# First stage of a fused attention and FFN kernel: row maximum taken with the bias sum, key blocks and values placed by POOL

## What is computed

```
xn = layernorm(x)                              # [32, 128, 128]
q  = xn @ Wq          -> 16 heads of 8
k  = ctx @ Wk         -> 4 groups of 8, each serves 4 heads
v  = ctx @ Wv         -> 4 groups of 8
ct = cumsum(deltas)
bias = w * log1p(abs(ct[:, None] - ct[None, :])) + (1 - mask) * -1e9
s  = q k^T / sqrt(8) + bias                    # 16 heads x 128 x 128 per batch
p  = softmax(s)
x1 = x + (p v) @ Wo
z  = layernorm(x1)                             # input of the main stage
out = x1 + main_stage(z)
```

## Time and profile before

| | us |
|---|---|
| median of three runs | 3308.8 (3306.87 to 3309.24) |
| span of the profiled execution, first to last instruction | 3304.7 |
| what the median has beyond that span | 4.1 |
| first score matmul of the first stage | starts at 17.2 |
| score matmuls of the stage's slots 3 to 32 | start at 35.97 to 292.58 |
| busy share of the whole span | PE 95%, DVE 87%, ACT 81%, POOL 74% |

### The profile page before, as it was taken

One profiled execution on the slowest core, in us unless ns is written; L12 is line 12 of the kernel. 1 busy time (PEld: TensorE's weight loads), 2 busy tenths in 40 slices (PEclk: granted clock), 3 DMA queues, 4 the chain that ended last, 5 costly groups with the idle time before them and its releaser, 6 DMA issues.

```text
span 3304.7 us, 181505 instructions
## 1 busy us (share of the span) xinstructions
PE 3125.4 (95%) x71268; PEld 2192.5 (66%) x71268; DVE 2884.0 (87%) x6045; ACT 2663.4 (81%) x5440; POOL 2447.9 (74%) x2673
## 2 busy tenths in 40 slices
PE   6776899999999999999999999999999999999996
PEld 4443567676667676676767667676676767667665
DVE  7886789999899999899999899998899999899984
ACT  6886678888788888788888788888788888788874
POOL 3333778888788888788888778787787878788883
PEclk9988999999999999999999999999999999999997
DMA  3000112122222222222222212122221212212121
GB/s 79 8 7 10 47 51 59 50 59 71 67 56 53 56 53 77 63 54 55 54 55 74 68 50 59 50 59 77 57 59 50 59 50 77 66 50 59 50 58 50
DMA packets 150374, 182.24 MB, mean 55 GB/s; under 512 B 51572, under 2 KB 74162, under 8 KB 149554
## 3 DMA queue, kind: packets, MB, share of 16 engines
q1 hardware_dynamic: 150322, 181.55, 21.2%
HBM read 21.32 MB, written 2.10 MB: 7 GB/s over the span
## 4 chain that ended last, share of the span: by engine, by line
PE 57%; issue 13%; DVE 10%; ACT 10%; POOL 5%; SPq 1%; DVEq 1%; DMA 1%; ACTq 1%; POOLq 0%
PE bank L1252 13%; PE bank L1339 8%; PE bank L1322 7%; PE bank L1262 5%; PE bank L1363 5%; PE bank L1270 3%; PE bank L1290 3%; ACT L798 3%; DVE tb L966 3%; ACT P L774 3%; PE bank L1392 2%; ACT gl L766 2%; POOL qk L524 2%; DVE bank L1075 2%; PE bank L1400 2%
## 5 line engine op out<-in xcount | busy, mean ns | idle before, releaser
L533 POOL TENSOR_TENSOR qk<-qk,rn 128x512 f32<-128x512 f32 x768 | 803.0, 1046 | 356.8 <-DVE rn L985 356.8
L524 POOL TENSOR_TENSOR qk<-ta,tb 128x512 f32<-128x512 f32 x768 | 978.6, 1274 | 2.5 <-DVE tb L966 2.5
L1252 PE MATMUL bank<-wqkv,zsT 128*128 128x512 f32 x1536 | 819.9, 617 | 25.4 <-ACT vt L705 12.3
L963 DVE TENSOR_TENSOR ta<-bank,rot 128x512 f32<-128x512 f32 x768 | 527.5, 687 | 116.1 <-ACT sq L688 87.4
L966 DVE TENSOR_TENSOR tb<-bank,rot 128x512 f32<-128x512 f32 x768 | 523.0, 681 | 0.0
L1068 DVE TENSOR_REDUCE bank<-sq 128x32 f32<-128x2048 f32 x192 | 440.6, 2295 | 25.1
L688 ACT ACTIVATE sq<-bank 128x512 f32<-128x512 f32 x768 | 445.2, 611 | 14.8 <-PE bank L1252 12.1
L696 ACT ACTIVATE qkT<-bank 128x512 f32<-128x512 f32 x768 | 396.6, 602 | 57.1 <-PE bank L1290 56.9
L1363 PEld LDWEIGHTS bank<-wo,oT 128*128 128x128 f32 x3072 | 375.4, 193 | 92.4 <-issue 92.4
L743 ACT ACTIVATE znT<-bank,small 128x128 f32<-128x128 f32 x192 | 87.9, 458 | 431.8 <-PE bank L1383 431.8
L564 POOL TENSOR_TENSOR P<-P,rowsum 128x512 f32<-128x512 f32 x384 | 392.9, 1045 | 20.0 <-DVE rowsum L1083 20.0
(11 more groups left out here) (131 smaller groups left out, 5740.6 us busy)
## 6 DMA issues: line engine op xcount, KB each, us to landing
vs<-vt SPq DMA_DIRECT2D x1152, 128.0 KB, 2.4
wqkv<-L_ffn_Wqkv SPq DMA_DIRECT2D x6, 1024.0 KB, 5.0
zm<-zm SPq DMA_DIRECT2D x192, 31.8 KB
wqkv<-L_ffn_Wqkv SPq DMA_DIRECT2D x6, 512.0 KB, 3.7
wo<-L_ffn_Wo SPq DMA_DIRECT2D x6, 512.0 KB, 4.0
z_sb<-x SPq DMA_DIRECT2D x4, 512.0 KB, 5.1
ctxb<-ctx SPq DMA_DIRECT2D x32, 64.0 KB, 1.8
w<-L_ffn_W SPq DMA_DIRECT2D x6, 341.0 KB
```

Of the source, the lines that this page charges most:

```text
L524: g.tensor_tensor(o, i0, i1, ALU.add).then_inc(s["g_add"], 1)
L533: g.tensor_tensor(q3, q3, r3, ALU.mult).then_inc(s["g_qk"], 1)
L963: v_.tensor_tensor(ta[:, c].rearrange("p (h d) -> p h d", d=DH), bank[j % 2][:, :].rearrange("p (h d) -> p h d", d=DH), rot[:, o:o + 64].u ...
L1252: t_.matmul(bank[j % 2][:, :], zsT[:, pu, :], wqkv[:, 512 * j:512 * j + 512], start=True, stop=True).then_inc(s["p_qk"], 1)
```

## The change

- `add_bias` and `maximum` become `bias_max`: per head one `tensor_tensor_reduce` of 128x128, which writes the sum of scores and bias to `XP` and the maximum over the row to one column of `xmax`. `xmax` gets two buffers.
- POOL subtracts the maxima of all four groups, in four instructions, each after its group of `bias_max`.
- ACT takes the exponentials of heads 8 to 15 in one instruction as those of 0 to 7, with no bias operand.
- ACT copies queries, keys and values of A out of bank 6 in one instruction of 288 columns to `qkvx`; the factor 1/sqrt(8) moves into the block mask `blk`.
- POOL makes `kblk` and `vaug` of A from `qkvx`, at the end of its slot.
- Two waits of PE before the transposes of A fall away, and ACT's copy waits for `vaug` of two batches before.

```
-c[:, C_BLK:C_BLK + XR] = (r[:, None] // XD) % XR == np.arange(XR)[None, :]
+c[:, C_BLK:C_BLK + XR] = ((r[:, None] // XD) % XR == np.arange(XR)[None, :]) * np.float32(XSCALE)
...
 POOL
-subtract(0)
-subtract(1)
+for gr in range(XG):
+    subtract(gr)          # waits x_add of group gr; 128x512 each
 if D_on:
     wait(pool, "x_ve", count(1, D, 1, B))
     g.tensor_tensor(rstd[:, 0:1], ve[:, 0:1], half_neg[:, 0:1], ALU.pow).then_inc(s["x_rstd"], 1)
     g.tensor_copy(x1_sb[:, bass.ds(D * E, E)], x1cur[:, :]).then_inc(s["x_store"], 1)
 if A1_on:
     deltas_of(A1, (k + 1) % 2)
+if A_on:
+    wait(pool, "x_q", count(1, A, 1, B))
+    wait(pool, "x_S", count(4, A - 2, 4, B))
+    g.tensor_tensor(kblk[:, pA, :].rearrange("p (r t) -> p r t", r=XR),
+                    qkvx[:, pA, S:2 * S].unsqueeze(1).to_broadcast([128, XR, S]),
+                    blk.unsqueeze(2).to_broadcast([128, XR, S]), ALU.mult).then_inc(s["x_kblk"], 1)
+    wait(pool, "x_O", count(1, A - 2, 1, B))
+    pool.nop(nofuse=True)
+    g.tensor_copy(vaug[:, pA, :, 0:XD], qkvx[:, pA, 2 * S:].rearrange("p (g d) -> p g d", g=XG))\
+        .then_inc(s["x_vaug"], 1)
...
 ACT, exponent(j)
-if j == 0:
-    wait(act, "x_sub", count(2, Bt, 2, B))
-    ins = a_.activation(pr, pr, ACT.Exp)
-else:
-    wait(act, "x_max", count(2, Bt, 2, B))
-    for h in range(8, 16):
-        pr = XP[:, pB, 128 * h:128 * h + 128]
-        ins = a_.activation(pr, pr, ACT.Exp, bias=xmax[:, h:h + 1])
+wait(act, "x_sub", count(4, Bt, 2 * j + 2, B))
+pr = XP[:, pB, 1024 * j:1024 * j + 1024]
+ins = a_.activation(pr, pr, ACT.Exp)
...
-a_.activation(qT[:, pA, :], bank[6][:, 0:128], ACT.Copy, scale=XSCALE).then_inc(s["x_q"], 1)
+wait(act, "x_vaug", count(1, A - 2, 1, B))
+a_.activation(qkvx[:, pA, :], bank[6][:, 0:2 * S + XG * XD], ACT.Copy).then_inc(s["x_q"], 1)
...
 DVE
-add_bias(0) ... add_bias(3)
-maximum(0)
+bias_max(gr), for gr in 0 to 3:
+    wait(dve, "x_S", count(4, Bt, gr + 1, B))
+    wait(dve, "x_sub", count(4, Bt - 2, gr + 1, B))
+    dve.nop(nofuse=True)
+    for h in range(4 * gr, 4 * gr + 4):
+        c = slice(S * (h % 4), S * (h % 4) + S)
+        ins = v_.tensor_tensor_reduce(XP[:, pB, S * h:S * h + S], bank[gr][:, c], bias[:, pB, :],
+                                      1.0, LOWEST, ALU.add, ALU.max, xmax[:, pB, h:h + 1])
+    ins.then_inc(s["x_add"], 1)
...
-maximum(1)
...
-wait(dve, "x_q", ...); v_.tensor_tensor(kblk ...)
...
-wait(dve, "x_O", ...); v_.tensor_copy(vaug ...)
...
 PE
-t_.matmul(bank[gr][:, :], qT[r, pB, :], kblk[r, pB, :], start=True, stop=True)
+t_.matmul(bank[gr][:, :], qkvx[r, pB, 0:S], kblk[r, pB, :], start=True, stop=True)
...
-wait(pe, "x_kblk", count(1, A - 1, 1, B))
-wait(pe, "x_vaug", count(1, A - 1, 1, B))
```

More of the change, by code:

```diff
@@ L42 @@
 MASKED = -(2.0 ** 120)
+LOWEST = -3.0e38
 C_ID, C_SH, C_TRI, C_ROT, C_MASK, C_SEL, C_BLK, C_END = 0, 128, 256, 384, 640, 704, 768, 772
@@ L161, in build @@
         cxT = sb("cxT", [128, 2, 2 * S])
-        qT = sb("qT", [128, 2, S])
+        qkvx = sb("qkvx", [128, 2, 2 * S + XG * XD])
         kblk = sb("kblk", [128, 2, XR * S])
@@ L168, in build @@
         bias = sb("bias", [128, 2, S])
-        xmax = sb("xmax", [128, XH])
+        xmax = sb("xmax", [128, 2, XH])
         xrs = sb("xrs", [128, XH])
@@ L190, in build @@
             "x_xn", "x_dc", "x_A1", "x_cxT", "x_dabs", "x_ln", "x_bias", "x_A2", "x_q", "x_kblk", "x_vaug", "x_S",
-            "x_add", "x_max", "x_sub", "x_exp", "x_PT", "x_PTc", "x_O", "x_Oc", "x_OT", "x_rs", "x_attn", "x_aT",
+            "x_add", "x_sub", "x_exp", "x_PT", "x_PTc", "x_O", "x_Oc", "x_OT", "x_rs", "x_attn", "x_aT",
             "x_aTc", "x_y", "x_x1", "x_store", "x_bn", "x_agg", "x_ve", "x_rstd", "z_ready",
@@ L469, in xslot, with subtract @@
                 A1, A1_on = part(n, -1, B)
+                A, A_on = part(n, 0, B)
                 Bt, B_on = part(n, 1, B)
                 D, D_on = part(n, 3, B)
-                pB = (k - 1) % 2
-                def subtract(i):
+                pA, pB = k % 2, (k - 1) % 2
+                def subtract(gr):
                     if B_on:
[L477 to L480, removed]
+                        wait(pool, "x_add", count(4, Bt, gr + 1, B))
+                        pr = XP[:, pB, 512 * gr:512 * gr + 512].rearrange("p (h q) -> p h q", q=S)
+                        mx = xmax[:, pB, 4 * gr:4 * gr + 4].unsqueeze(2).to_broadcast([128, 4, S])
+                        g.tensor_tensor(pr, pr, mx, ALU.subtract).then_inc(s["x_sub"], 1)
                 def deltas_of(A, pA):
@@ L625, in exponent @@
                     if B_on:
-                        if j == 0:
-                            wait(act, "x_sub", count(2, Bt, 2, B))
-                            pr = XP[:, pB, 0:1024]
-                            ins = a_.activation(pr, pr, ACT.Exp)
-                        else:
-                            wait(act, "x_max", count(2, Bt, 2, B))
-                            for h in range(8, 16):
-                                pr = XP[:, pB, 128 * h:128 * h + 128]
-                                ins = a_.activation(pr, pr, ACT.Exp, bias=xmax[:, h:h + 1])
+                        wait(act, "x_sub", count(4, Bt, 2 * j + 2, B))
+                        pr = XP[:, pB, 1024 * j:1024 * j + 1024]
+                        ins = a_.activation(pr, pr, ACT.Exp)
                         ins.then_inc(s["x_exp"], 1)
@@ L855, in xslot, with bias_max @@
                 xc = bass.ds(D * E, E)
-                def add_bias(gr):
+                def bias_max(gr):
                     if B_on:
                         wait(dve, "x_S", count(4, Bt, gr + 1, B))
+                        wait(dve, "x_sub", count(4, Bt - 2, gr + 1, B))
                         if gr == 0:
@@ L863, in add_bias @@
                             wait(dve, "x_bias", count(1, Bt, 1, B))
[L864 to L881, removed]
-                maximum(0)
+                        dve.nop(nofuse=True)
[4 more added lines that the diff above has]
+                        ins.then_inc(s["x_add"], 1)
+                bias_max(0)
+                bias_max(1)
+                bias_max(2)
+                bias_max(3)
                 if D_on:
@@ L887, in xslot @@
                     v_.reciprocal(xrs[:, :].rearrange("p (g r) -> p r g", g=XG), o4[:, :, :, XD]).then_inc(s["x_rs"], 1)
-                if D_on:
                     wait(dve, "x_rs", count(1, D, 1, B))
@@ L903, in xslot @@
                     v_.tensor_tensor(x1cur[:, :], bank[4][:, 0:128], z_sb[:, xc], ALU.add).then_inc(s["x_x1"], 1)
[L904 to L910, removed]
                 if D_on:
@@ L923, in xslot @@
                                             ALU.mult, ALU.add).then_inc(s["x_bias"], 1)
-                    wait(dve, "x_O", count(1, A - 2, 1, B))
-                    wait(dve, "u_v1", 1)
-                    v_.tensor_copy(vaug[:, pA, :, 0:XD], bank[6][:, 256:288].rearrange("p (g d) -> p g d", g=XG))                        .then_inc(s["x_vaug"], 1)
                 if D_on:
@@ L1152, in xscores @@
                         r = slice(32 * gr, 32 * gr + 32)
-                        t_.matmul(bank[gr][:, :], qT[r, pB, :], kblk[r, pB, :], start=True, stop=True)\
+                        t_.matmul(bank[gr][:, :], qkvx[r, pB, 0:S], kblk[r, pB, :], start=True, stop=True)\
                             .then_inc(s["x_S"], 1)
```

## The result

The changed kernel takes 3362.5 us (3360.6 to 3366.5), the kernel before 3308.1 in the same comparison: a ratio of 1.0169, 95% interval 1.0154 to 1.0183. It is 54 us slower. The forecast was slower with 3400 in a range of 3350 to 3460: the direction and the mechanism came out, the size was 1.7 times too large, and the result lies near the low end of the range.

What follows compares the result with a forecast made beforehand. It took a closed loop of 8.27 us to bound the first stage's 8.85 us slot; plus 0.74 and 2.34 made 11.93, times 29 plus 89 us, plus 2 for the ends and 4.1 beyond the span: 3400 us, range 3350 to 3460.

Steps and rivals of the forecast that it cites:

- The bound: First stage: a closed loop from scores to next scores, not an engine, sets the 8.85 us slot, 29 times.
- The rival with the engines' busy time: First stage: DVE's busy time sets the slot, so it shrinks by 1.4 us, to 3268 us; 7 in 100.
- Key blocks on POOL: A's keys wait behind D's rstd on POOL: 3.25 us in place of 0.91, plus 2.34 a slot.
- Bias sum and maximum together: DVE's sixteen per-head reductions at 0.267 us each take 4.27 us in place of 3.53, plus 0.74 a slot.
- The forecast's own low end: Free maximum and half of the 0.58 us: plus 1.72 a slot; 3361 us, opened to 3350.
- The part of a slot over the loop at full clock: Mean slot's 0.58 us beyond the loop, put to TensorE's lower clock and slots without a key wait; kept as before.
- The loop of 8.27: Sum in us of one first-stage slot's steps, from scores back to scores, in the kernel before.
- The keys' term: First-stage loop: plus 2.34 us a slot for A's key blocks made on POOL.
- the ends of the stage: First slots without a D and the last score slot: plus 2 us for dearer sums.
- Second maximum: 1.12 us of DVE behind the scaling, beside the loop, covered by PE's projections; its removal gives nothing.
- subtractions: Two more POOL instructions of 1.04 us; POOL keeps pace with the sums, nothing on the path.
- exponentials: ACT's eight instructions of 2.44 us per slot become one of 1.05; ACT gains 1.4 us, off the loop.

Runs made afterwards that it cites:

- experiment 3: Changed kernel with A's keys and values back on DVE, copied from the bank as before; maxima, subtractions and exponentials stay changed: 3308.5 us, ratio 0.9997.
- experiment 1: Changed kernel with A's key blocks and values on POOL moved ahead of rstd, the copy of x1cur and dcur: 3313.6 us, ratio 1.0014.
- experiment 6: Changed kernel with the copy of x1cur and dcur on POOL moved from ahead of the key blocks to behind the values: 3349.9 us, ratio 1.0118.
- experiment 7: Experiment 3's kernel with, on DVE, keys ahead of x1cur and D's reciprocal and scaling ahead of the last group of sums: 3271.7 us, ratio 0.9892.
- experiment 8: Experiment 7's kernel with D's reciprocal and scaling ahead of the last two groups of sums instead of one: 3245.5 us, ratio 0.9804.
- experiment 2: Kernel before with only ACT's 288-column copy and A's keys and values on POOL at the end of its slot: 3364.5 us, ratio 1.0169.
- experiment 4: Experiment 3's kernel with D's four transposes issued twice more on PE, inside its wait for DVE's scaling: 3290.6 us, ratio 0.9941.

## Why the prediction was right in kind and too high

- **The bound.** Right: a loop and not an engine. The removal of a fifth of DVE's and ACT's work in experiment 3 moved the time by nothing, and moves inside the loop (experiments 1, 6, 7, 8) moved it by what the loop says, experiment 1 by 13 us less. The rival with the engines' busy time is out: DVE at 52% would have meant a faster stage.
- **Key blocks on POOL.** Right: plus 2.34 forecast; 3.13 in place of 0.91, plus 2.22, in the slot shown (2.23 in the means). Experiments 1 and 2 show that it is this step and its place in the order.
- **Bias sum and maximum together.** The step that was mis-sized. It was put as 0.20 plus 0.067 for a result written apart, 4.27 us for sixteen, plus 0.74 in the loop. The trace has 3.38, minus 0.15. The read of the maximum is an instruction of its own, as the forecast allowed, but it runs beside the start of the next head's and adds 0.011 and not 0.067. The difference, 0.89 us in 29 slots, is 26 us of the 37 by which the forecast was high. The forecast's own low end had this case, a free maximum, and gave 3361 before it was opened to 3350. The Trainium skill, "VectorE: DVE Perf Modes", section on two Vector instructions with no wait between them, says that such an operation is two instructions; the trace agrees, with 432 reads of 84 ns each. The price that the forecast quoted as an estimate from "Vector Engine (DVE) Microarchitecture Reference", section 5.2, some 75 ns for each of the two, is seen once and not twice: a head takes 0.211 against the 0.20 worked out for a plain sum, which has one such fixed part in it already. By the estimate it would have been 0.283.
- **The part of a slot over the loop at full clock.** Taken as 0.58 as before; in the changed kernel it is 10.93 less 10.46, 0.47, though the granted clock fell from 0.91 to 0.86. The term was near for a reason that it did not give. The loop of 8.27 was put together from two slots, with the 1.36 between scores and first sum from the later one; the slot itself had 1.98 there and the mean is 1.54. Of the 0.58, about 0.2 us lay in that step, 0.2 in PE's transpose and projections, and 0.23 in front of the scores, where PE still had the values' product. The last part went in the changed kernel (0.47 to 0.24 in the table), as the forecast says of that product and yet does not take off; in its place the first sum comes 0.25 later behind the scores. The two cancel by luck.
- **The rest.** The keys' term was 0.12 too high, 3 us; the ends of the stage were put at plus 2 and gave 1; the median lies 1.5 us beyond the profiled span and not 4.1; 5 us of the stage's 61 came back behind it. By the landmarks of the two first profiles that is 0.7 between the last scores and the first residual sum of the main stage, 3.7 in the main stage and 0.7 in the tail. That no part of the main stage changes was assumed; whether the 3.7 belong to the program or to the execution stays open.
- **Second maximum, subtractions, exponentials.** Put at nothing and worth nothing in the changed kernel; the last subtraction ends at 152.55 and `rstd` starts at 154.28. What was missed is that less work on the other engines can cost: PE's two waits become one, with a lower clock behind it (experiments 3 and 4). That the earlier exponentials on ACT do this is argued; no run changes them alone. By the table it is worth the 0.27 us by which experiment 3's slot is longer than before. What the sums gain is taken back by the late first sum, whose cause stays open.

## What to carry to other kernels

Where queues are in order and no engine is full, add up the closed loop from one slot's first instruction to the next one's, judge each edit by what it does to that sum, and check it against the mean of many slots; the busy shares did not tell it here. An operation moved to an idle engine inherits every wait that stands ahead of it there, and is worth moving only to a place where those are already met. Before work is made cheaper, look at the order: the same instructions ran at 9.12 and 7.07 us a slot.

## What the runs showed of the hardware

- Reading out a row maximum after a reduction of 128 columns has a record of 84 ns, but the pair repeats every 0.211 us. That is 0.011 us more than the 0.20 of a plain sum of 128 columns, which is an estimate from the sums of 512 columns.
- With a longer single wait of PE (2.0 us in place of 1.0 and 0.9) the mean granted clock was 0.87 in place of 0.91 (experiment 3); repeated transposes, 1.1 us, in that wait brought it to 1.00, and made the kernel 18 us faster, with more work (experiment 4).
- The scores' eight matmuls took 1.14 us in some slots at the full clock and 1.45 to 1.49 in others. A wait for the keys does not decide it: 1.14 stands behind a wait of 2.28 us in the changed kernel (at 354.01), and 1.49 in a row without a wait in experiment 8 (at 156.37). What does is open.
